# Values of an mLSTM with v as the stationary operand, a scan layer as a pipeline, and key projections moved behind the affinities

## What is computed

```
x = x + gated_scan(ln(x))                       # layer 1, scan
x = x + mlstm(ln(x), ctx, ctx)                  # layer 1, 4 heads of 32
x = x + moe(ln(x))                              # 8 experts, top 1 with a capacity rule
x = x + scan(ln(x))                             # layer 2: sigmoid(g) * tanh(v), decay from sigmoid(d)
x = x + attention(ln(x), ctx, ctx)              # 16 heads of 8, causal
x = x + moe2(ln(x))                             # 8 experts, top 2, SwiGLU
```

```
c = q @ (k.T / sqrt(dh)) * d                    # d: causal decays, s x s
n = max(sum(c, -1), exp(-m))
h = c / (n + eps) @ v
```

## Time and profile before

| | |
|---|---|
| median of 3 runs | 698.41 us (696.13 to 700.05) |
| profiled execution, its own time | 698.65 us |
| span of its profile | 696.9 us |
| granted TensorE clock, mean | 0.778 of 2.4 GHz |
| busy: PE, PEld | 514.7 us (74%), 404.9 us (58%) |
| busy: DVE, POOL, ACT | 340.1 us (49%), 222.4 us (32%), 211.0 us (30%) |
| chain that ended last | PE 51%, DVE 22%, issue 12%, POOL 4%, ACT 4%, DMA 3% |

### The profile page before, as it was taken

The page is one execution under the profiler, slowest core; times in us unless marked ns, Lnnn a source line. Parts: engine busy times, 40 slices in busy tenths (PEclk is TensorE's granted clock), DMA queues, the critical chain, the costliest instruction groups (busy, mean ns, idle before and its releaser), DMA issues.

```text
span 696.9 us, 12794 instructions
## 1 busy us (share of the span) xinstructions
PE 514.7 (74%) x4709; PEld 404.9 (58%) x4709; DVE 340.1 (49%) x1045; ACT 211.0 (30%) x431; POOL 222.4 (32%) x333
## 2 busy tenths in 40 slices
PE   3367789997769995864879999899784875574910
PEld 1135568886359981623856666666563774574910
DVE  4646535677633314066234556566842454342632
ACT  3020553322115650432523444344231331121300
POOL 4501035652731008111103333233166006244044
PEclk9577955555659996797967999999775888795965
DMA  9970100000168111001300111111021401331132
GB/s 241 346 220 1 36 26 2 1 0 1 49 114 56 37 44 45 17 1 45 140 1 1 18 17 16 17 17 9 9 42 51 102 16 53 107 88 36 47 84 63
DMA packets 114716, 38.60 MB, mean 55 GB/s; under 512 B 76768, under 2 KB 112224, under 8 KB 114016
## 3 DMA queue, kind: packets, MB, share of 16 engines
q1 hardware_dynamic: 111440, 31.30, 19.1%
q0 software_dynamic: 3072, 6.30, 3.1%
q10 hardware_dynamic: 144, 0.19, 0.1%
HBM read 22.45 MB, written 15.34 MB: 54 GB/s over the span
## 4 chain that ended last, share of the span: by engine, by line
PE 51%; DVE 22%; issue 12%; POOL 4%; ACT 4%; DMA 3%; another core or an unknown queue 2%; DVEq 1%; SPq 0%; POOLq 0%; ACTq 0%
PE bank L1221 6%; PE bank L1384 5%; PE bank L1097 4%; PE bank L1366 4%; DVE first_max_of L1876 4%; PE bank L1400 3%; PE bank L1168 3%; PE bank L1179 3%; PE bank L1264 2%; PE bank L1098 2%; PE bank L1279 2%; DVE XN L1434 2%; POOL rstd L641 2%; DVE first_max_of L1875 2%
## 5 line engine op out<-in xcount | busy, mean ns | idle before, releaser
L754 POOL TENSOR_SCALAR_AFFINE_SELECT score_room<-score_room 128x256 f32<-128x256 f32 x128 | 48.2, 408 | 127.1 <-ACT score_room L918 127.1
L918 ACT ACTIVATE score_room<-bank 128x1152 f32<-128x1152 f32 (+1 forms) x43 | 48.3, 1124 | 100.9 <-PE bank L1282 97.4
L641 POOL TENSOR_TENSOR rstd<-vareps,power 128x4 f32<-128x4 f32 x24 | 24.5, 1019 | 123.4 <-DVE vareps L1426 123.2
L1384 PE MATMUL bank<-sel_room 128*128 128x128 f32 x368 | 56.2, 302 | 0.5 <-issue 0.2
L1400 PE MATMUL bank<-ctxT,h_room 128*128 x184 | 33.7, 312 | 29.2 <-issue 19.7
L1875 DVE TENSOR_REDUCE first_max_of<-bank 128x3 f32<-128x384 f32 (+1 forms) x43 | 23.9, 555 | 60.1 <-PE bank L1369 60.1
L1384 PEld LDWEIGHTS bank<-sel_room 128*128 128x128 f32 x368 | 51.2, 215 | 2.4 <-issue 0.9
L776 POOL DMA_INDIRECT w_room<-part_outputs,f_rows x32 | 30.8, 962 | 59.0 <-DMA part_outputs<-sel_room 49.8
L1400 PEld LDWEIGHTS bank<-ctxT,h_room 128*128 128x128 f32 x184 | 28.0, 218 | 31.3 <-issue 31.2
L1888 DVE TENSOR_TENSOR h_room<-bank,h_room 128x256 f32<-128x256 f32 x46 | 19.5, 424 | 50.1 <-issue 27.5
L1279 PE MATMUL bank<-QM,w_room 32*128 32x256 f32 x256 | 38.0, 434 | 6.1 <-DVE QM L1865 5.2
(11 more groups left out here) (276 smaller groups left out, 1151.7 us busy)
## 6 DMA issues: line engine op xcount, KB each, us to landing
w_room<-in_w SPq DMA_DIRECT2D x2, 2048.0 KB, 11.2
part_rows<-OV SPq DMA_DIRECT2D x2, 1472.0 KB, 16.7
part_outputs<-sel_room SPq DMA_DIRECT2D x10, 256.0 KB, 2.3
scan_room<-in_w SPq DMA_DIRECT2D x1, 2048.0 KB, 7.8
slot_rows<-OV SPq DMA_DIRECT2D x1, 1472.0 KB, 17.0
score_room<-slot_rows SPq DMA_DIRECT2D x5, 256.0 KB, 5.2
slot_outputs<-XNT SPq DMA_DIRECT2D x5, 256.0 KB, 2.3
w_room<-part_rows SPq DMA_DIRECT2D x5, 256.0 KB, 4.2
```

What stands on the lines that cost most here:

```text
L641: pool.tensor_tensor(rstd[:, t0:t1], vareps[:, t0:t1], power[:, 0:1].to_broadcast([P, CT]), ALU.pow).then_inc(rstd_ready, 1)
L754: last = pool.affine_select(cells, cells, [[0, 2], [1, P]], ALU.is_ge, 0.0, base=0, channel_multiplier=-1)
L918: act.activation(pT[:, v % RING, 0:n, :], banks(3, n)[:, :, 0:CUT], ACT.Exp, scale=float(AD) ** -0.5).then_inc(e_p, 1)
L1384: last = pe.matmul(ps[n % 2][:, k * P:(k + 1) * P], w12_now[:, n % 2, k * P:(k + 1) * P], turned, start=True, stop=True)
```

## The change

1. mLSTM: v (64 of its columns, of which 33 count) becomes the stationary operand and `cT` moves, 256 and 128 columns at a time; two heads go side by side into the two 64-row halves of bank 6. The result has tokens along the free axis, so ACT copies the bank to `OB` (`copy_values`) and PE turns it by four transposes into bank 7, from where DVE divides. The decays of batch b + 1 are issued before the turn of batch b - 1.
2. Keys: chunk 0 is projected between the affinities and the `earlier` product, chunk 1 after the mean, ahead of the transposes for the ranks; chunks 2 and 3 after the projections of chunks 0 and 1 of the scan layer. `KT` is split over `sel_room` and the first half of `w_room`; half of the queries goes to the second half of `w_room`.
3. Scan layer: `layer_norm` is split into `norm_stats` and `norm_apply` on DVE, with a scan between them, and the queries of a chunk start while later chunks still scan.

The core of the diff:

```diff
+            def copy_values(b):
+                act.wait_ge(b_pv, b + 1)
+                if b >= 1:
+                    act.wait_ge(b_ot, b)
+                act.activation(OB, ps[6][:], ACT.Copy).then_inc(b_ov, 1)
...
+                if u % 2 == 1 and u >= 2:
+                    copy_values(u // 2 - 1)
+            copy_values(B - 1)
...
+            copy_heads(KT[0], 0, (6, 7), e_kt, e_ktc, col("one_row"))
+            copy_heads(KT[0], 1, (6, 5), e_kt, e_ktc, col("one_row"))
...
             def b_values(b):
...
-                for h in range(NH):
-                    weights = cT[:, (NH * b + h) % (2 * NH), :]
-                    for i in range(2):
-                        n = NH * i + h
-                        o = ps[6 + b % 2][:, n * HW:n * HW + HD + 1]
-                        pe.matmul(o, weights[:, i * P:(i + 1) * P], vaug[:, 2 * b, h, :], start=True, stop=(i == 0))
-                    last = pe.matmul(o, weights[:, S:CUT], vaug[:, 2 * b + 1, h, :], start=False, stop=True)
+                else:
+                    pe.wait_ge(b_ov, b)
+                for q in range(2):
+                    for i in range(2):
+                        for f in range(2):
+                            h = 2 * q + f
+                            at = ((2 * b + i) * NH + h) * (HD + 1)
+                            last = pe.matmul(ps[6][HW * f:HW * (f + 1), q * S + i * P:(q + 1) * S], v_room[:, at:at + HW],
+                                             cT[:, (NH * b + h) % (2 * NH), i * S:CUT if i else S], start=(i == 0), stop=(i == 1))
+                last.then_inc(b_pv, 1)
+            def b_turn_values(b):
+                pe.wait_ge(b_ov, b + 1)
...
+                else:
+                    pe.wait_ge(b_div, b)
+                for q in range(2):
+                    for i in range(2):
+                        n, m = 2 * i + q, 2 * q + i
+                        last = pe.transpose(ps[7][:, n * P:(n + 1) * P], OB[:, m * P:(m + 1) * P], ident)
                 last.then_inc(b_ot, 1)
+            b_decays(0)
             for b in range(B):
                 b_scores(b)
                 if b >= 1:
                     b_values(b - 1)
+                if b + 1 < B:
+                    b_decays(b + 1)
+                if b >= 1:
+                    b_turn_values(b - 1)
...
+            pe.wait_ge(b_div, B)
+            project_keys(0, (6, 7))
             pe.wait_ge(c_oh, 1)
...
             pe.wait_ge(c_sum, 1)
+            pe.wait_ge(e_ktc, 4)
             pe.matmul(ps[7][:, 0:1], ones[:], asum[:], start=True, stop=True).then_inc(c_mean, 1)
+            project_keys(1, (6, 5))
...
             pe.wait_ge(c_yc, C_GROUPS)
+            d_project(0, turn_xn(0))
+            project_keys(2, (6, 7))
+            d_project(1, turn_xn(1))
+            project_keys(3, (6, 7))
+            d_output(0)
+            d_project(2, turn_xn(2))
+            d_output(1)
+            d_project(3, turn_xn(3))
+            pe.wait_ge(e_ktc, 4 * C)
+            project_queries(0, turn_xn(0))
+            d_output(2)
+            project_queries(1, turn_xn(1))
+            d_output(3)
+            project_queries(2, turn_xn(2))
+            project_queries(3, turn_xn(3))
...
+            d_arrive(0)
+            norm_apply(0)
+            d_arrive(1)
+            norm_apply(1)
+            d_arrive(2)
+            d_scan_chunk(0)
+            norm_apply(2)
+            d_arrive(3)
+            d_scan_chunk(1)
+            norm_apply(3)
+            d_leave(0)
+            d_scan_chunk(2)
+            norm_apply(0)
```

More of the change, by code:

```diff
@@ L326, in build @@
         b_pv = sem("b_pv")
+        b_ov = sem("b_ov")
+        b_ot = sem("b_ot")
         b_div = sem("b_div")
@@ L830, in _, with spread, copy_heads @@
             act.activation(bsum[:], ps[7][:, 0:D], ACT.Copy).then_inc(c_bsumc, 1)
+            def copy_values(b):
[3 more added lines that the diff above has]
+                act.activation(OB, ps[6][:], ACT.Copy).then_inc(b_ov, 1)
+            def spread(bank, c, q):
+                return (bank[:].rearrange("p (g m t) -> p m t g", g=4, t=NA),
+                        slice(BC * NA // OG * c, BC * NA // OG * (c + 1)), slice(4 * q, 4 * q + 4))
+            def copy_heads(room, c, pair, asked, copied, bias):
+                for q in range(4):
+                    act.wait_ge(asked, 4 * c + q + 1)
+                    src, slots, parts = spread(ps[pair[q % 2]], c % 2, q)
+                    dst = room[:, slots, :].rearrange("p m (t g) -> p m t g", g=QG)[:, :, :, parts]
+                    act.activation(dst, src, ACT.Identity, bias=bias).then_inc(copied, 1)
             def square_heads(b):
@@ L878, in _ @@
                 last.then_inc(c_act, 1)
-            def spread(bank, c, q):
-                return (bank[:].rearrange("p (g m t) -> p m t g", g=4, t=NA),
-                        slice(BC * NA // OG * c, BC * NA // OG * (c + 1)), slice(4 * q, 4 * q + 4))
-            for k in range(4 * C):
-                c, q = divmod(k, 4)
-                act.wait_ge(e_kt, k + 1)
-                src, slots, parts = spread(ps[6 + k % 2], c, q)
-                act.activation(KT[:, slots, :].rearrange("p m (t g) -> p m t g", g=QG)[:, :, :, parts], src, ACT.Identity,
-                               bias=col("one_row")).then_inc(e_ktc, 1)
-            cp = copy_xnt(3)
+            cp, cp_next = copy_xnt(3), copy_xnt(4)
             for c in range(C):
@@ L900, in _ @@
                 act.activation(state[:, c % 2, :], ps[4][:], ACT.Sigmoid, bias=col("bd")).then_inc(d_act, 1)
-            cp = copy_xnt(4)
+                if c < 2:
+                    copy_heads(KT[1], 2 + c, (6, 7), e_kt, e_ktc, col("one_row"))
             for c in range(C):
-                cp(c)
-                for q in range(4):
-                    k = 4 * c + q
-                    act.wait_ge(e_q, k + 1)
-                    src, slots, parts = spread(ps[2 + k % 4], c % 2, q)
-                    act.activation(QT[c // 2][:, slots, :].rearrange("p m (t g) -> p m t g", g=QG)[:, :, :, parts], src, ACT.Copy).then_inc(e_qc, 1)
+                cp_next(c)
+                copy_heads(QT[c // 2], c, (6, 7), e_q, e_qc, 0.0)
             for step in range(LAST):
@@ L1104, in _, with by_head, project_keys @@
                     b_values(b - 1)
+                if b + 1 < B:
+                    b_decays(b + 1)
+                if b >= 1:
+                    b_turn_values(b - 1)
             b_values(B - 1)
+            b_turn_values(B - 1)
+            def by_head(w, moving, c, q, bank):
+                tokens = moving[:, c * CW:(c + 1) * CW].rearrange("p (m j t) -> p j m t", j=OG, t=NA)
+                for g in range(4 * q, 4 * q + 4):
+                    for j in range(OG):
+                        last = pe.matmul(bank[OW * j:OW * (j + 1), (g - 4 * q) * P:(g - 4 * q + 1) * P], w[:, g, :], tokens[:, j], start=True, stop=True)
+                return last
+            def project_keys(c, pair):
+                for q in range(4):
+                    pe.wait_ge(e_ktc, 4 * c + q - 1 if q >= 2 else 4 * c)
+                    by_head(awk, ctxT, c, q, ps[pair[q % 2]]).then_inc(e_kt, 1)
             xt = XNT[0]
@@ L1751, in d_residual, with d_arrive, d_leave @@
                 dve.tensor_tensor(ch, ps[5][:].rearrange("p (t d) -> p t d", d=D), ch, ALU.add).then_inc(d_add, 1)
[L1753 removed]
+            def d_arrive(c):
                 c_residual(c)
                 dve.wait_ge(c_acc, c + 1)
[L1756 to L1768 removed]
+                norm_stats(c)
+            def d_leave(c):
+                d_residual(c)
+                dve.wait_ge(d_add, c + 1)
+                norm_stats(c)
+            d_arrive(0)
[11 more added lines that the diff above has]
+            norm_apply(0)
+            d_leave(1)
+            d_scan_chunk(3)
+            norm_apply(1)
+            d_leave(2)
+            norm_apply(2)
+            d_leave(3)
+            norm_apply(3)
             def best_two(h):
```

95 lines of the change are left out of this document (31 added, 64 removed).

## The result

| | before | changed |
|---|---|---|
| median of 4 runs | 698.7 us (696.13 to 700.05) | 669.14 us (664.5 to 671.12) |
| profiled execution, own time | 698.65 us | 671.12 us |
| span | 696.9 us | 669.4 us |
| granted clock, mean | 0.778 | 0.805 |

What follows compares the result with a forecast made beforehand. Bounds: PE's values in the mLSTM, a path over PE, DVE and POOL in the routing, keys between experts and attention. 698.65 - 14 (mLSTM) + 5.5 (routing) - 17 (scan layer) = 673.1, so 673 us; range 659 to 686.

Steps and rivals of the forecast that it cites:

- mLSTM, -14 predicted: mLSTM: values with narrow stationary v shorten the 7.70 us batch; -14 us over 8 batches, ends -9 and -19.
- both levels by turns: mLSTM: PE's clock alternates between low (6.6 us a batch) and high (5.3), so the middle, -14 us, was taken.
- the 5.3 us: mLSTM: batch period at the high clock, including gaps between dependent instructions; 2.4 us less than now, 19 over 8 batches.
- DVE is the bound: mLSTM at the high clock: DVE limits the batch, with 3.21 us in a light one and 5.72 when norming a chunk.
- The drain between shapes: mLSTM: TensorE's drain at changes of matmul shape was claimed to cost nothing visible.
- The rule of the Trainium skill: mLSTM: changing tiling mode drains TensorE; one more change per batch would make the gain 1.8 us smaller.
- The serial rival: mLSTM values: the two column groups don't run side by side, 6.0 us a batch; total 702 us, slower; chance 5%.
- Routing, +5.5 predicted: Routing: key chunks 0 and 1 placed there delay scatters and rank rows; +5.5 us, ends +0.2 and +8.5.
- half of 5.7: Routing: rank-row stalls of 5.7 us beside the scatters shrink as rows fall half behind the scatters' end.
- Second layer, -17 predicted: Experts to attention: the scan layer's new order starts queries 17.0 us earlier; -17 us, bounds -21 and -12.
- keys 2 crawl until about 283.8, then need 5: Scan layer: key chunk 2, after projection 0, is slow until about 283.8, then needs 5 us, ending at 289.
- The third rival: Experts to attention: key chunks 2 and 3 and DVE's fixed order give back all but 6 us; 684 us, 9%.

Runs made afterwards that it cites:

- totals first: Changed kernel with the `earlier` and ones products and the mean moved ahead of key chunk 0 in the routing: 690.75 us in a single run.
- without pipeline: Changed kernel with key chunks 2 and 3 ahead of the scan layer and its old order on PE, ACT and DVE: 690.53 us in a single run.
- keys second: Changed kernel with key chunks 0 and 1 moved from the routing to the second layer, ahead of projection 0: 669.91 us in a single run.
- both combinations: Changed kernel with key chunk 1 in the second layer and POOL's norm one batch later, 633.47 us; the same with key chunk 0 behind the block totals, 626.9 us.

## Why the prediction was right

**mLSTM, -14 predicted, -12.5 measured.** PE at the low clock: 6.6 us a batch predicted, 6.17 measured (values 2.83 for 3.0, turn 1.06 for 1.0, decays and scores somewhat shorter). The clock: I expected both levels by turns, and so it came, 0.50 in the first batch and in the last full window (129.03), 0.70 to 1.00 between them. Light batches beat the 5.3 us (4.35, 4.61); those in which DVE takes the statistics of a chunk (6.96, 6.70) or writes its norm (5.65) missed it. The step that was off is "DVE is the bound" for the first two: there it is a ring over DVE's statistics, POOL's rstd and the selection behind it, as POOL's norm moved by a batch showed; 3.4 us. The drain between shapes costs nothing visible: the batch at 94.59 has all its changes of shape, and PE is busy 6.17 of 6.17 us, though the ends of matmuls in a profile are modelled and could hide a short one. The rule of the Trainium skill (TensorEngine Tiling (Array Packing), Key Properties), by which the gain would have been 1.8 us smaller, has no idle time here to stand on; the ring is more than enough for the missing 1.5 us. The serial rival fell by a wide margin (2.83 us in place of 6.0): two groups of 64 columns run side by side, in either order.

**Routing, +5.5 predicted, +5.8 measured.** Chunks 5.82 and 3.84 (5.46 and 4.5 predicted). Two errors cancel, so the match is luck. The first rank product came 6.8 us later, not 8.5 (170.75 - 154.69 = 16.1 after the affinities, before 175.77 - 166.47 = 9.3): the `earlier` product came 4.2 us late (4.0 predicted), chunk 1 took 0.7 less than foreseen, and from the first rank transpose (L1185) to the first rank product there are 5.3 us in place of 6.5, which the sum had left as they were. And the halts of the rank rows, by the 17.2 us that they take alone, were 6.4 before (175.77 to 199.36; 5.7 in the prediction) and are 5.4 now: only 0.9 went, where the step wanted half of 5.7. 6.8 - 0.9 = 5.9.

**Second layer, -17 predicted, -22.3 measured.** Set on the same clock, by the experts' last copy, the prediction had projection 0 over at 278.5 (278.2 measured), keys 2 at 289 (284.0), queries at 311.6 (304.9), attention at 332.8 (327.5). The step that failed is "keys 2 crawl until about 283.8, then need 5": 58 of the 128 records ran at once, and when the last gather had been issued (275.1 in the changed kernel's own time, 1.3 us sooner after the experts than before) only 64 were left, 2.08 us, so the chunk took 5.9 us in place of 10.5. That is 5.0 of the 5.3 us that the stage is off; up to the queries 1.7 more are gained, and about as much is lost again between queries and attention (22.7 us in place of 21.1).

**Sum.** 673 predicted, 669.14 measured, inside 659 to 686.

**The third rival** (the pipeline doesn't pay) was wrong on the chip of the result, with 22.3 us in place of 6, and right in its reason: most of the keys' time was the gathers', not the keys'. On the chip where the records don't crawl it seems to hold as a whole: by the estimate above keys and pipeline together change the time by about 0 (between -2 and +3 us). How much of the 22.3 us the order of the scan layer earns apart from getting the keys out of the gathers' way stays open. The prediction took the crawl of the earlier trace rows for a property of the program; it is one of the chip as well, and the 16.5 us that keys and pipeline bring together (22.3 - 5.8), of 29.5, hang on it.

## What to carry to other kernels

Where PE's records come singly with "issue" ahead of them, look at what POOL sends: 512 key records took 37 us here beside indirect gathers and 15 beside plain transfers. What waits for such work can be moved ahead of it, and a part that fits can be done before the first indirect DMA, where it ran at full speed. A narrow operand can go to the side of the weights: 16 records of 256 and 128 moving columns replaced 24 with 33, and with the four transposes took 3.9 us a batch in place of 5.1 at the low clock. And a gain that rests on one contention should be measured on more than one chip: the same change gave 4.3% on one and 1.9% on another.

## What the runs showed of the hardware

- While POOL issues indirect DMAs, PE's short fp32 records fall from one in 30 ns (128 in 3.83 us) to one or two in a us, in every profile but the three of one chip: with totals first, 26 in the 14 us from 173.04; without pipeline, 13 in the 8 us from 264.55. After a wait the first 36, 36 and 48 still ran whole (keys second, no pipeline, totals first), and behind projection 0 the first 58 (changed kernel). Why, no run tested. On the one chip there was none of it (64 in 1.95 us between gathers, 28 rank records in 14.52 us between scatters), though POOL sent one every 1.27 us as elsewhere. What sets that chip apart is open.
- Not only records are late there. With keys second, PE's last record of the first chunk ends at 246.99, but ACT's copy that waits for it starts at 251.85, 5.0 us after ACT was free. On the chip without the crawl (both combinations' key chunk 1, at the same place) the fourth copy follows the third in 0.19 us.
- Plain transfers of the same size on SP's queue, 16 in 11.07 us, don't cause it: 512 records in 15.17 us.
- Matmuls of two 64-column groups overlap in either order of the groups: 2.83 and 2.88 us at the low clock, 1.52 and 1.57 at the high one, where 3072 moving columns of full width take 2.84.
- In the mLSTM with the old values, 33 moving columns to a weight load, the clock was 0.50 with PE busy without a gap, and again with the values put back. With 256 and 128 columns it rose after one batch of 6.17 us without idle time, was 0.70 to 1.00 over the next five and back at 0.50 from 129.03.
